# The next batch's keys chosen behind the maxima and the division of block 6, with scaling and masking in one VectorE instruction

## What is computed

```python
qb = q.reshape(B, H, M, BS, HD).mean(axis=3)
kb = k.reshape(B, H, M, BS, HD).mean(axis=3)
c = jnp.einsum('bhmd,bhnd->bhmn', qb, kb) * SCALE
k_keep = max(1, int(round(M * (1.0 - SPARSITY))))
thresh = jax.lax.top_k(c, k_keep)[0][..., -1:]
block_mask = (c >= thresh) | jnp.eye(M, dtype=bool)
...
scores = jnp.where(tmask, scores, -jnp.inf)
probs = jax.nn.softmax(scores, axis=-1)
out = jnp.einsum('bhqk,bhkd->bhqd', probs, v)
...
x = x + _L0_attn_ref(_layernorm(x, axis=-1), ...)
x = x + _L0_ffn_ref(_layernorm(x, axis=-1), ...)
```

## Time and profile before

| | |
|---|---|
| median of 3 runs | 933.33 us (932.52 to 937.24) |
| profiled execution | 938.29 us, of which the span is 936.6 us |
| TensorE matmuls busy | 865.7 us, 92% of the span |
| VectorE busy | 553.3 us, 59% |
| ScalarE busy | 459.8 us, 49% |
| POOL busy | 182.0 us, 19% |
| mean granted TensorE clock | 0.983 |

### The profile page before, as it was taken

One profiled execution on the slowest core, in us unless ns is written; L12 is line 12 of the kernel. 1 busy time (PEld: TensorE's weight loads), 2 busy tenths in 40 slices (PEclk: granted clock), 3 DMA queues, 4 the chain that ended last, 5 costly groups with the idle time before them and its releaser, 6 DMA issues.

```text
span 936.6 us, 24244 instructions
## 1 busy us (share of the span) xinstructions
PE 865.7 (92%) x9638; PEld 578.2 (62%) x9638; DVE 553.3 (59%) x1554; ACT 459.8 (49%) x740; POOL 182.0 (19%) x183
## 2 busy tenths in 40 slices
PE   3687899999999999999999999999999999999995
PEld 2465676666667666666656666665766666576662
DVE  7355747475665847566574847567474756736321
ACT  1332474635546373644637364563736456373641
POOL 5601111212121121212111121212112121211111
PEclk8798999999999999999999999999999999999998
DMA  7351342515344260625336161533516153340110
GB/s 207 87 148 39 117 133 77 162 30 164 92 130 131 79 178 14 185 70 144 117 82 179 28 187 51 149 110 100 161 50 175 41 150 98 108 141 2 57 57 14
DMA packets 96021, 99.40 MB, mean 106 GB/s; under 512 B 8968, under 2 KB 82704, under 8 KB 95904
## 3 DMA queue, kind: packets, MB, share of 16 engines
q1 hardware_dynamic: 93168, 85.09, 32.2%
q0 software_dynamic: 2544, 12.58, 4.2%
q10 hardware_dynamic: 192, 0.13, 0.1%
HBM read 48.10 MB, written 28.71 MB: 82 GB/s over the span
## 4 chain that ended last, share of the span: by engine, by line
PE 55%; DVE 15%; issue 11%; DMA 8%; SPq 4%; ACT 3%; POOL 2%; ACTq 1%; another core or an unknown queue 1%; POOLq 0%; DVEq 0%
PE y_ps L403 13%; PE s_ps L310 8%; PE o_ps L346 5%; PE s_ps L259 4%; DVE rmax L661 4%; PE s_ps L261 4%; DMA selected<-kv_table,index 4%; PE s_ps L260 3%; DMA kv<-kv_chosen 3%; SPq L1120 3%; PE s_ps L335 3%; ACT hid L949 2%; PE a_ps L376 2%; PE v_ps L326 2%; PE a_ps L268 2%
## 5 line engine op out<-in xcount | busy, mean ns | idle before, releaser
L403 PE MATMUL y_ps<-hid,w2s 128*128 128x512 f32 x480 | 240.8, 602 | 0.0
L913 ACT ACTIVATE prob<-s_ps 128x1024 f32<-128x1024 f32 x128 | 131.2, 1025 | 202.3 <-PE s_ps L335 202.3
L661 DVE TRANSPOSE_TENSOR_REDUCE rmax<-s_ps 128x16 bf16<-128x512 f32 x256 | 168.6, 701 | 59.0 <-PE s_ps L310 55.0
L949 ACT ACTIVATE hid<-s_ps,b1s 128x512 f32<-128x512 f32 x256 | 171.2, 689 | 35.5 <-PE s_ps L261 35.0
L310 PE MATMUL s_ps<-qdiag,kv 64*128 64x512 f32 x768 | 132.8, 450 | 5.9 <-DMA qdiag<-qpair 2.8
L259 PE MATMUL s_ps<-xnhi,w1hi 128*128 128x512 f32 x256 | 111.6, 436 | 1.5
L1049 POOL TENSOR_TENSOR yT<-yT,gate_cols 128x512 f32<-128x512 f32 x48 | 61.5, 1282 | 259.0 <-DVE gate_cols L757 258.5
L670 DVE TENSOR_REDUCE nmax<-v_ps 128x64 bf16<-128x256 bf16 x128 | 54.0, 422 | 97.0 <-PE v_ps L326 97.0
L310 PEld LDWEIGHTS s_ps<-qdiag,kv 64*128 64x128 f32 x768 | 85.2, 252 | 32.9 <-ACT hid L949 10.6
L906 ACT COPY vaug<-v_ps 128x128 f32<-128x128 f32 x128 | 34.1, 266 | 138.3 <-PE v_ps L319 129.9
L261 PE MATMUL s_ps<-xnhi,w1lo 128*128 128x512 f32 x256 | 100.8, 394 | 0.0
(11 more groups left out here) (149 smaller groups left out, 1078.3 us busy)
## 6 DMA issues: line engine op xcount, KB each, us to landing
gate_cols<-gates SPq DMA_DIRECT2D x64, 256.0 KB, 5.1
kv_table<-stage SPq DMA_DIRECT2D x16, 768.0 KB, 3.9
kv<-stage SPq DMA_DIRECT2D x16, 768.0 KB, 6.5
kv_chosen<-selected SPq DMA_DIRECT2D x15, 768.0 KB, 5.3
kv<-kv_chosen SPq DMA_DIRECT2D x15, 768.0 KB, 4.9
qdiag<-qpair SPq DMA_DIRECT2D x504, 16.0 KB
xs<-in_x SPq DMA_DIRECT2D x16, 256.0 KB, 4.4
out_x<-x SPq DMA_DIRECT2D x16, 256.0 KB, 4.7
```

The lines of the kernel that those rows point to most:

```text
L403: ins = pe.matmul(dst[:], w2s[:, n, :], hid[:, n, :], start=(c == 0), stop=(c == C - 1))
L661: v.tensor_reduce(rmax[m % 2][:, :, half * P // 2:half * P // 2 + HH].rearrange("p k h -> p h k"), s_ps[m % 2][:, half * N:(half + 1) * N] ...
L913: act.activation(prob[m % 2][:].rearrange("p h s -> p (h s)"), s_ps[m % 2][:], ACT.Exp, scale=SCALE).then_inc(exped, 1)
L949: act.activation(hid[:, k, :], up_ps[up_bank(k)], ACT.Gelu, bias=b1s[:, k:k + 1]).then_inc(gelued, 1)
```

## The change

In `a_select` the scaling of the products (`tensor_scalar`, PSUM to `crow`) and the multiplication with the mask `mine_of` (`tensor_tensor`, SBUF) become one `scalar_tensor_tensor` that reads the products from PSUM and the mask from SBUF. In VectorE's loop the call of `a_select` moves, for batches 1 to 14, from behind `nmax` of block 6 to behind `block_max` of block 7 and the division of the third pair (`o_rows`). In batch 0 it stays where it was. The other engines' programs are unchanged.

```diff
             def a_select(b):
                 j = b % 2
                 v.wait_ge(bank_a.full, bank_a.at["products", b])
-                v.tensor_scalar(crow[:].rearrange("p m n -> p (m n)"), a_ps[:, 0:M * M], 1.0 / (BS * BS), SCALE,
-                                ALU.mult, ALU.mult).then_inc(bank_a.free, 1)
+                v.scalar_tensor_tensor(crow[:].rearrange("p m n -> p (m n)"), a_ps[:, 0:M * M], SCALE / (BS * BS),
+                                       mine_of[:].rearrange("p m n -> p (m n)"), ALU.mult, ALU.mult).then_inc(bank_a.free, 1)
                 v.wait_ge(bank_a.free, bank_a.at["products", b])
-                v.wait_ge(dve_step, step(v.tensor_tensor(crow[:], crow[:], mine_of[:], ALU.mult)))
                 v.wait_ge(dve_step, step(v.tensor_reduce(cown[:], crow[:].rearrange("p m n -> p n m"), AXX, ALU.add)))
...
                         if m == products_at:
                             a_qk(max(q_total, k_total))
-                        if m == products_at + 1:
+                        if b == 0 and m == products_at + 1:
                             tied = a_select(b + 1)
...
                     if m in (2, 4, 6):
                         o_rows(b, (m - 2) // 2)
+                    if b >= 1 and b + 1 < B and m == products_at + 1:
+                        tied = a_select(b + 1)
                     if b >= 2 and m % 2:
                         c_gated(b - 2, m // 2)
```

## The result

The changed kernel takes 984.98 us at the median (four runs, 983.91 to 987.67); the kernel before takes 932.92 beside it. The ratio is 1.0553, with a 95% interval of 1.0512 to 1.0593: 5.5% slower. The forecast was 982, with a range of 957 to 996.

A forecast was written before the change was run, and what follows sets the result against it. The prediction took each batch to be bound by both TensorE and the transfer of the chosen keys. Late keys (32.9 us) plus clock falls (16) made 49, so 933.3 + 49 = 982 us, range 957 to 996.

The forecast's parts named there:

- The bound: At the next batch's first scores, TensorE and the transfer of the chosen keys arrive together; slack taken as 0.1 us.
- The fused instruction: In the choice on VectorE, it takes 0.23 us, the multiply having waited for POOL; `crow` to `index` becomes 1.44 us.
- The move: On VectorE, `index` comes 2.30 us later a batch, 4.40 in batch 1; less slack, the scores' delay totals 32.9 us.
- TensorE's gain: At `weighted` and the next stall, TensorE is some 0.85 us earlier, but idles 3.1 us a batch at the scores.
- The clock: TensorE's clock falls behind three in four of the 14 waits, losing 1.5 us each, 16 us in all.
- one in two on record: Of two idle stretches at the start of the trace, one had a clock fall; basis for taking three in four.
- the 2.83 us gap: Idle stretch ending at 28.66, clock 1.00; spoke for the rival that the clock holds, 966 or 961 us, chance 0.24.
- The sum: Whole kernel: 32.9 + 16 = 49 us, added to the median of the runs, 933.3, giving 982 us.

The follow-up runs named there:

- fused_old_place: Kernel before with the fused instruction, the choice left directly behind `nmax` of block 6: 929.42 us, ratio 0.9889 to the kernel before.
- moved_only: Kernel before with the call of `a_select` at the new place, scaling and multiply still two instructions: 995.80 us, ratio 1.0615 to the kernel before.
- before_take_late3: Kernel before with SP's load of the chosen keys issued three placements of q later, choice not moved: 988.35 us, ratio 1.0503.
- after_filled: Changed kernel with 12 unread matmuls ahead of the next batch's first scores, where TensorE waits: 974.23 us, ratio 1.0384 to the kernel before.
- before_take_late1: Kernel before with SP's load of the chosen keys issued one placement of q later, choice not moved: 949.94 us, ratio 1.0123.
- after_take_first: Changed kernel with SP's load of the chosen keys issued ahead of five placements of q: 954.44 us, ratio 1.0168 to the kernel before.

## Why the prediction was right

**The bound.** TensorE and the keys arrive together: shown from both sides. Keys one placement later cost 1.2%. Keys 1.3 us earlier gain 0.4%, since TensorE alone needs 20.08 us of the mean 20.36. The prediction took the slack as 0.1 us a batch. From `index` on, the path to the scores takes 20.36 - 2.31 = 18.05 us before and 19.24 - 1.41 = 17.83 after, so it was 0.2.

**The fused instruction.** Forecast 0.23, measured 0.21; `crow` to `index` 1.44 and 1.41. That the 0.86 us of the multiply were a wait for POOL is shown by fused_old_place and moved_only: either the operand or the moment was changed, and the instruction took 0.22 us in both.

**The move.** `crow` was forecast 3.17 us later in the turn (490.15 against 486.98); the one turn that is not long has 36.99 - 33.80 = 3.19. Without the clock a turn grew by (19.24 - 20.36) + 3.19 = 2.07 us, against 2.30 - 0.1 = 2.2 forecast. In batch 1, from its first scores to those of batch 2, it was 59.97 instead of 55.21 us, so 4.76 more against 4.3. Together 13 x 2.07 + 4.76 = 31.7, where the term of the prediction was 32.9. before_take_late3 shows that it is the late keys that cost this and not what else was moved.

**TensorE's gain.** The 0.93 us at `weighted` are gone, and what TensorE gained by it went into the wait, as forecast: 42.1 / 14 = 3.0 us a batch, 3.1 forecast. In batch 8, counted from the start of `x`, TensorE was ready for the scores after 530.77 - 512.73 = 18.04 us, and 506.3 - 488.26 = 18.04 was forecast.

**The clock.** Falls behind three in four of the 14 waits at 1.5 us, 16 us in all, were the choice between none and all of them. Measured were twelve of the thirteen turns in the table, each 1.4 to 1.6 us: 13 x (38.41 - 36.99) = 18.5 us. The fourteenth wait, 2.94 us long, stands ahead of batch 15 and cost nothing, since the matmuls behind it run at full speed:

```profile
878.22 1.03 PE L310 MATMUL s_ps<-qdiag,kv 64*128 64x512 f32 x6 [2.94 <-DMA kv<-kv_chosen]
...
880.55 0.40 PE L261 MATMUL s_ps<-xnhi,w1lo 128*128 128x512 f32 x1
```

So there were twelve falls in 14 waits. The mechanism and the size of one fall were right, and the number of them low. That the number came so near is in part luck, for the "one in two on record" behind it was read from too few rows. The prediction looked at the stretch of the 2.83 us gap alone, where the clock is 1.00. The next two stretches of the kernel before are:

```profile
30.00:35.00 5.00, 0.01 (x1) 0.00 (x0) 1.45 (x2) 0.00 (x0) 4.37 (x5) 0.61 0.30 82
35.00:40.00 5.00, 4.40 (x37) 2.71 (x41) 1.77 (x4) 2.73 (x4) 4.84 (x6) 0.50 0.16 31
```

The clock did fall there, behind a second idle stretch of 5.59 us that follows at once, so that gap was no evidence that the clock holds. after_filled shows that the falls come from the idle wait: with the wait filled there are none.

**The sum.** 31.7 + 18.5 = 50.2 us, forecast 49, between the medians 52. The two spans differ by 45.6 only, because the profiled execution before had its first scores of batch 1 at 73.42 us from the start and the one after at 68.78. That difference of 4.64 lies ahead of everything that was changed. It is a wait in front of the first `row_max` of batch 0, first in the kernel before, then in the changed one:

```profile
35.60 0.37 PE L326 MATMUL v_ps<-idn,rmax 128*128 128x128 bf16 x2 [5.59 <-ACT vaug L906]
```

```profile
30.91 0.37 PE L326 MATMUL v_ps<-idn,rmax 128*128 128x128 bf16 x2 [1.14 <-DVE rmax L660]
```

In the profiles of all kernels here this wait lies between 1.0 and 5.7 us, so single executions can differ by over 4 us without any change. The prediction had put its sum on the median for another reason and was spared this by chance.

## What to carry to other kernels

Before an instruction is moved past others because these are waited for, follow what it starts itself, through every queue, to the place where that is needed, and compare the landing with the start there: here 0.2 us of slack stood against 2.3 us of delay. Fusing was worth 1.1% where it took an operand out of SBUF, beside POOL's work, and it needed no move. Where a wait for a transfer can't be avoided, reckon with its second price, the clock behind it; and look first at the order of the queue that issues the transfer, which gave back more here than filling the wait.

## What was not expected of the hardware

The clock does not go by the length of the last wait alone. In before_take_late1 the turn behind a wait of 1.57 us (it ends at 731.45) was 1.6 us longer than the others. In after_take_first a wait of 2.00 us (it ends at 244.76) cost nothing, nor did those of 2.97 and 2.94 us in the changed kernel that end at 591.48 and 878.22, while the turn behind the one of 2.96 us that ends at 533.73 was long. What else decides was not settled.

In fused_old_place the hold by POOL passes to the next instruction of VectorE with two operands in SBUF and lasts until POOL's ends: 0.12 us in `cties` in place of 0.64 in the multiply. The Trainium skill, "SBUF — State Buffer", section "Who interferes with whom", says that a VectorE instruction with two SBUF inputs contends with a GpSimd instruction that reads SBUF. It also says that one with at most one SBUF input doesn't contend, outside the two-port modes. These traces agree, with 0.22 us for the fused instruction inside `xnlo`, against 0.86 for the multiply that has both inputs in SBUF.

SP takes 1.07 us for each placement of q that it issues while the write of the keys is under way (5.35 for five), and 0.73 behind the load of the keys (3.63 for five, in after_take_first). That load is a transfer of the same size and under way then too, so a large transfer beside them is not the whole reason; the rest was not looked into.
